# Low parts of the rotated groups made by VectorE one step later in place of GpSimd, and the attention ratio by `tensor_scalar` in place of `scalar_tensor_tensor`

## The chip, the cores and the metric

The kernel runs on one core of one Trainium2 chip. The metric is the time of one execution on the device in microseconds (us); the kernel before has a median of 1994.56 us over three runs (1994.23 to 1994.79). A measurement of this kernel can tell about 0.2% (4 us) from no change.

## What is computed

Eight sequences of 512 tokens by 512 features go through one layer: differential attention with rotary embedding, group normalisation, an output projection, a residual and a layer norm, and then a mixture of eight experts of which each token takes two, with another layer norm. The change is in the attention, of which this is the core (16 heads, 4 groups of keys and values, 32 columns to each half of a head):

```python
q1, q2 = _rope(q1, cos, sin), _rope(q2, cos, sin)
k1, k2 = _rope(k1, cos, sin), _rope(k2, cos, sin)
...
s1 = jnp.einsum('bhtd,bhsd->bhts', q1, k1) * scale + mask
s2 = jnp.einsum('bhtd,bhsd->bhts', q2, k2) * scale + mask
a1 = jax.nn.softmax(s1, axis=-1)
a2 = jax.nn.softmax(s2, axis=-1)
diff = a1 - lam * a2
out = jnp.einsum('bhts,bhsd->bhtd', diff, v)
```

Here `_rope` multiplies by the cosine, and adds the neighbour columns (swapped in pairs) times the sine.

## The kernel before

The attention of the eight sequences (batches) is a software pipeline of 48 steps for each batch: four key/value groups (kv) with 12 units each. A unit is one tile of 128 query rows and, for the tiles 0 and 1, two heads, for the tiles 2 and 3 one head; so 16 of a batch's 48 units have two heads (steps 0 to 3, 12 to 15, 24 to 27, 36 to 39). The order of the work is written out by hand: every engine has its own program, loops over the steps and does, in each step, its part of several units that are at different ages. Engines wait for each other by semaphores that count.

In step s, TensorE makes the scores of unit s into `S` (line 660, mask 664), transposes the mixed probabilities of unit s-3 (675), does a share of the next projection into `prep` (642 to 644), tasks of the batch before, and every few steps the products with the values (688, 691). VectorE does, in this order: `scaled_out` in some steps (1081), `maxes` of unit s (1042), `inverse_sums` of unit s-1 (reciprocals, 1050), `mix` of unit s-2 (1073: `mixed = expd_2 * rho + expd_1`, one `scalar_tensor_tensor` a head), `ratios` of unit s-1 (1059: `rho = -lambda * sum_1 / sum_2`, for the heads of the unit in one `scalar_tensor_tensor`), and then, in the steps of a table, `rotate` (1034, 1035), statistics and tasks of the batch before. ScalarE makes the exponentials (856) and copies the transposes (868).

The projections of queries and keys come in groups of 128 columns, ten a batch (`SEQ`: q2, q3, k1, q4, q5, q6, q7, k0, q0, q1; the last batch has seven). `FILL_STEPS` says in which steps a group's four parts are projected; the last of the four is the step in which it is rotated: 2, 5, 8, 12, 15, 18, 23, 32, 35, 38. A group then goes this way:

- in its step, VectorE multiplies `prep` by the cosine into `turned` (1034) and shuffles it into `swapped` (1035), which frees `prep`;
- GpSimd, in the same step of its own program, multiplies `swapped` by the sine (555) and adds it to `turned` (557);
- two steps later, ScalarE copies `turned` rounded into the high part of `parts` (953, `high_part`), and GpSimd subtracts that from `turned` into the low part (562, `low_part`, waits for `hi_done`, adds to `lo_done`);
- SP stores the high part when `hi_done` says so, the low part when `lo_done` does (461), and when both stores have landed gathers the four blocks of 32 rows into `qT` or `kT` (472, `spread`). 

`turned` is a single buffer: `rotate` of the next group waits for `lo_done` of the group before. TensorE waits, in the first step of each kv (step 12 for the second), for the gathers of the groups that it needs; step 12 needs q2 and q3, which are rotated in steps 2 and 5. SP's queue is one program: while it waits for a low part, its later transfers (weights of the next groups, the residual's rows) stand behind it. GpSimd's program has, beside the rotations and low parts, the copies of the values (549) and the indirect DMAs that scatter the finished rows to the experts (578).

The rotation's three operations and the low part run on VectorE for the three groups of the preamble (1034, 1035, 1415, 1417, 1420). From about 1300 us on the experts and the combination follow, which the change does not touch.

## Time and profile before

| what | value |
|---|---|
| median of three runs | 1994.56 us |
| span of the profiled execution, from the first to the last instruction | 1982.6 us |
| median less span | 12.0 us |
| busy: PE, DVE, ACT, POOL | 1681.3, 1394.1, 1166.2, 578.0 us |
| low parts on POOL (562) | 77, mean 1293 ns |
| rotation on POOL (555, 557) | 77 each, mean 1287 and 1394 ns |
| ratios on DVE (1059) | 384, mean 307 ns |
| mixes on DVE (1073) | 512, mean 681 ns |

PE is TensorE, DVE VectorE, ACT ScalarE, POOL GpSimd, SP the queue of most DMAs. A row of a timeline has the start and the duration in us, the engine, the line of the kernel, the operation, the tile written and the tiles read (buffer numbers left out), the shapes, the count of merged instructions, and in brackets how long the engine was idle before it and what ended that. A row of groups has count, busy us and mean ns, then the idle time before. A row of a line has durations in ns (least, median, greatest). The profiled execution's time outside its span is not in the profile; the table has what the median leaves for it.

### The profile page before, as it was taken

Reading aid. Unit: us, or ns where it says so; the run is one execution under the profiler, and the core shown is the slowest. Engines: PE = TensorE matmul, PEld = TensorE weight load, DVE = VectorE, ACT = ScalarE, POOL = GpSimd, SP = SyncE. Lnnn points to the kernel's source line nnn. Section 1 sums busy time; section 2 is a strip of 40 time slices with the busy share of each in tenths; the row PEclk is TensorE's granted clock in tenths of the full one; section 3 lists DMA queues with packets and bytes.
Section 4 is the critical chain, followed back from the end, with each engine's and each line's share of the span. In section 5 each row is a group of like instructions: output and inputs, shape, how many; then the busy total and the mean of one; then the engine's idle time right before and its main releaser. Section 6 shows DMA issues by size and latency. Waiting matters only on the chain. (4 is left out here: it accounts for less than half of the span.)

```text
span 1982.6 us, 36940 instructions
## 1 busy us (share of the span) xinstructions
PE 1681.3 (85%) x9718; PEld 1251.6 (63%) x9719; DVE 1394.1 (70%) x3225; ACT 1166.2 (59%) x3388; POOL 578.0 (29%) x471
## 2 busy tenths in 40 slices
PE   4878898898899899889889889873999999999800
PEld 3556556656566655656656665543999999999700
DVE  4998888988888988888898898744333333333377
ACT  2777878877788788787887887832222222222133
POOL 0322322522432432241251252012533342100075
PEclk8999999999999999999999999985999999999955
DMA  8764755765574574484575566014533344433187
GB/s 280 229 169 128 202 139 139 213 170 150 170 202 120 160 207 124 133 232 125 149 229 144 139 203 179 24 71 175 164 118 118 109 127 148 132 95 94 65 258 250
DMA packets 141462, 311.40 MB, mean 157 GB/s; under 512 B 16608, under 2 KB 19296, under 8 KB 140160
## 3 DMA queue, kind: packets, MB, share of 16 engines
q1 hardware_dynamic: 111264, 231.64, 41.3%
q0 software_dynamic: 15072, 50.74, 7.7%
q10 hardware_dynamic: 14976, 27.27, 3.6%
q8 instruction: 65, 1.06, 0.2%
q14 instruction: 85, 0.70, 0.1%
HBM read 207.87 MB, written 101.71 MB: 156 GB/s over the span
## 5 line engine op out<-in xcount | busy, mean ns | idle before, releaser
L856 ACT ACTIVATE expd<-S,neg_max 128x128 f32<-128x128 f32 (+3 forms) x1024 | 530.9, 535 | 152.5 <-DVE neg_max L1042 151.3
L1042 DVE TENSOR_REDUCE neg_max<-S 128x2 f32<-128x768 f32 (+3 forms) x384 | 399.5, 1040 | 144.9 <-PE S L664 135.7
L1073 DVE SCALAR_TENSOR_TENSOR mixed<-expd,rho 128x384 f32<-128x384 f32 (+3 forms) x512 | 338.8, 681 | 0.0
L660 PE MATMUL S<-kT,qT 128*128 128x256 f32 (+2 forms) x1024 | 276.7, 373 | 30.0 <-DMA qT<-parts_rows 18.2
L675 PE MATMUL PTp<-ident,mixed 128*128 128x128 f32 x1280 | 211.7, 280 | 57.4 <-DVE mixed L1073 53.0
L868 ACT ACTIVATE probsT<-PTp 128x512 f32<-128x512 f32 (+2 forms) x384 | 205.2, 534 | 91.3 <-PE PTp L675 88.8
L1529 ACT ACTIVATE xT_hi<-xTp 128x512 fp32r<-128x512 f32 x72 | 43.1, 599 | 357.9 <-DVE yo L1710 352.0
L660 PEld LDWEIGHTS S<-kT,qT 128*128 128x128 f32 x1024 | 162.5, 193 | 132.5 <-issue 92.0
L722 PE MATMUL tail<-wo,ctxT 128*128 128x512 f32 x464 | 218.9, 595 | 0.3
L856 ACT ACTIVATION_READ_ACCUMULATOR expd<-S,neg_max 128x1 f32 x1024 | 216.7, 212 | 0.0
L555 POOL TENSOR_TENSOR swapped<-swapped,rope_t 128x512 f32<-128x512 f32 x77 | 99.1, 1287 | 397.2 <-DVE swapped L1035 397.2
L675 PEld LDWEIGHTS PTp<-ident,mixed 128*128 128x128 f32 x1280 | 139.6, 142 | 78.0 <-DVE mixed L1073 74.4
L562 POOL TENSOR_TENSOR parts<-turned,parts 128x512 fp32r<-128x512 f32 x77 | 99.6, 1293 | 271.1 <-ACT parts L953 271.1
L691 PE MATMUL O<-probsT,vals 128*64 128x256 f32 x1280 | 168.5, 393 | 0.0
L642 PE MATMUL prep<-xh,wqk 128*128 128x512 f32 x308 | 141.6, 460 | 7.2 <-DVE swapped L1035 7.1
L1710 DVE COPY yo<-Y 128x512 f32<-128x512 f32 x72 | 49.8, 691 | 121.2 <-PE Y L1654 121.2
L1787 POOL DMA_INDIRECT ya<-expert_out_rows,out_slots x64 | 68.9, 1076 | 208.4 <-PEq L1742 189.2
L664 PE MATMUL S<-maskb,identb 128*128 128x128 bf16 (+1 forms) x768 | 125.1, 245 | 0.0
L644 PE MATMUL prep<-xh,wqk 128*128 128x512 f32 x308 | 123.6, 401 | 0.0
L643 PE MATMUL prep<-xl,wqk 128*128 128x512 f32 x308 | 122.7, 398 | 0.0
L1689 DVE TENSOR_TENSOR xT_lo<-xTp,xT_hi 128x512 fp32r<-128x512 f32 x72 | 49.8, 691 | 100.9 <-ACT xT_hi L1529 100.9
L1059 DVE SCALAR_TENSOR_TENSOR rho<-sums,neg_lam,rsum 128x1 f32<-128x1 f32 (+1 forms) x384 | 117.8, 307 | 0.0
(245 smaller groups left out, 3632.7 us busy)
## 6 DMA issues: line engine op xcount, KB each, us to landing
qT<-parts_rows SPq DMA_DIRECT2D x256, 256.0 KB, 4.5
parts_rows<-parts SPq DMA_DIRECT2D x160, 256.0 KB, 2.8
wqk<-wqk_split SPq DMA_DIRECT2D x75, 512.0 KB, 6.1
xin<-expert_in_rows SPq DMA_DIRECT2D x72, 256.0 KB, 3.0
expert_out_rows<-yo ACTq DMA_DIRECT2D x72, 256.0 KB, 3.2
kT<-parts_rows SPq DMA_DIRECT2D x64, 256.0 KB, 4.2
x<-in_x SPq DMA_DIRECT2D x8, 1024.0 KB, 7.2
x_rows<-x SPq DMA_DIRECT2D x8, 1024.0 KB, 7.3
```

The source lines that it names most:

```text
L642: nc.tensor.matmul(prep[:], w[:, c, 0, :], xh[:, c, :], start=(c == 0), stop=False)
L643: nc.tensor.matmul(prep[:], w[:, c, 0, :], xl[:, c, :], start=False, stop=False)
L644: mm = nc.tensor.matmul(prep[:], w[:, c, 1, :], xh[:, c, :], start=False, stop=(c == DC - 1))
L660: nc.tensor.matmul(S[s % 2][:, k * slot:k * slot + w], qT[kv % 2][:, 2 * h + c, i * P:(i + 1) * P], kT[kv][:, c, 0:w], start=(k % per_bank ...
L664: mm = nc.tensor.matmul(bank[:, :, i * P:(i + 1) * P], identb[:], maskb[:].unsqueeze(1).broadcast_to([P, per_bank, P]), start=False, stop= ...
L675: mm = nc.tensor.transpose(PTp[:, o:o + P], mixed[sl % 3][:, a * 256 + j * P:a * 256 + (j + 1) * P], ident[:])
L691: mm = nc.tensor.matmul(O[half * HD:(half + 1) * HD, 0], vals[kv][:, j, :], probsT[i % 2][:, j, half], start=(j == 0), stop=(j == i), tile ...
L722: mm = nc.tensor.matmul(tail[:], ctxT[par][:, c, i * P:(i + 1) * P], wo[:, c, :], start=(c == 2 * first_q), stop=(c == FC - 1))
L856: ex = nc.scalar.activation(expd[s % 3][:, k * slot:k * slot + w], S[s % 2][:, k * slot:k * slot + w], ACT.Exp, bias=neg_max[s % 3][:, k:k ...
L868: nc.scalar.activation(probsT[i % 2][:, 0:i + 1, half:half + n, pair, :].rearrange("p j a q -> p a j q"), PTp[:, 0:w].rearrange("p (a j q) ...
L1042: nc.vector.tensor_reduce(neg_max[s % 3][:, 0:k], v, AX, ALU.max, negate=True).then_inc(max_ready, 1)
L1073: ins = nc.vector.scalar_tensor_tensor(out=mixed[sl % 3][:, a * 256:a * 256 + w], in0=e2, scalar=rr[:, i, h:h + 1], in1=e1, op0=ALU.mult, ...
```

## The change

GpSimd's `low_part` goes, and VectorE gets one, three steps after the group's step in place of two, ahead of the `rotate` of that step. And `ratios` becomes one `tensor_scalar` a head: its one tensor is the sum, its two scalars the other head half's reciprocal sum and -lambda, both read from memory, one number a partition.

```diff
             def body(b, first, second, last):
                 for s, kv, u in steps(b, first, last):
-                    for idx in fills(s, last, 2):
-                        if SEQ[idx][0] != "v":
-                            low_part(group_no(b, idx), half(b, idx))
                     for idx in fills(s, last, 0):
                         if SEQ[idx][0] != "v":
                             rope(group_no(b, idx), fill_no(b, idx), SEQ[idx][0])
...
+            def low_part(n, r2):
+
+                dve.wait_ge(hi_done, n + 1)
+                nc.vector.tensor_tensor(parts[r2][:, 1, :], turned[:], parts[r2][:, 0, :].bitcast(F32),
+                                        ALU.subtract).then_inc(lo_done, 1)
+
...
                 dve.wait_ge(rsum_step, u + 1)
-                nc.vector.scalar_tensor_tensor(out=rr[:, i, h0:h0 + nh], in0=L[:, i, 0, h0:h0 + nh],
-                                               scalar=neg_lam[:, 0:1], in1=Q[:, i, 1, h0:h0 + nh],
-                                               op0=ALU.mult, op1=ALU.mult).then_inc(rho_step, 1)
+                for h in heads:
+                    ins = nc.vector.tensor_scalar(rr[:, i, h:h + 1], L[:, i, 0, h:h + 1], Q[:, i, 1, h:h + 1],
+                                                  neg_lam[:, 0:1], ALU.mult, ALU.mult)
+                ins.then_inc(rho_step, 1)
...
+                    for idx in fills(s, last, 3):
+                        if SEQ[idx][0] != "v":
+                            low_part(group_no(b, idx), half(b, idx))
                     for idx in fills(s, last, 0):
                         if SEQ[idx][0] != "v":
                             rotate(group_no(b, idx), fill_no(b, idx), SEQ[idx][0])
```

VectorE, before, from the mix of step 4 to the maxima of step 6 (rows give line, operation, tiles and the shape written):

```order
L1073 SCALAR_TENSOR_TENSOR mixed<-expd,rho 128x256 x2
L1059 SCALAR_TENSOR_TENSOR rho<-sums,neg_lam,rsum 128x2
L1042 TENSOR_REDUCE neg_max<-S 128x2
L1050 RECIPROCAL rsum<-sums 128x2
L1073 SCALAR_TENSOR_TENSOR mixed<-expd,rho 128x256 x2
L1059 SCALAR_TENSOR_TENSOR rho<-sums,neg_lam,rsum 128x1
L1034 TENSOR_TENSOR turned<-prep,rope_t 128x512
L1035 STREAM_SHUFFLE swapped<-prep 128x512
L1042 TENSOR_REDUCE neg_max<-S 128x2
```

The same stretch of VectorE with the change:

```order
L1077 SCALAR_TENSOR_TENSOR mixed<-expd,rho 128x256 x2
L1063 TENSOR_SCALAR rho<-sums,rsum,neg_lam 128x1 x2
L1045 TENSOR_REDUCE neg_max<-S 128x2
L1053 RECIPROCAL rsum<-sums 128x2
L1077 SCALAR_TENSOR_TENSOR mixed<-expd,rho 128x256 x2
L1063 TENSOR_SCALAR rho<-sums,rsum,neg_lam 128x1
L1037 TENSOR_TENSOR parts<-turned,parts 128x512
L1031 TENSOR_TENSOR turned<-prep,rope_t 128x512
L1032 STREAM_SHUFFLE swapped<-prep 128x512
L1045 TENSOR_REDUCE neg_max<-S 128x2
```

The ratio of step 4, of a unit of two heads, has become two instructions, that of step 5 is still one; and the low part of q2 (`parts`) stands between the ratio and the rotation of q3.

GpSimd, before, the first two groups of the loop:

```order
L555 TENSOR_TENSOR swapped<-swapped,rope_t 128x512
L557 TENSOR_TENSOR turned<-turned,swapped 128x512
L562 TENSOR_TENSOR parts<-turned,parts 128x512
L555 TENSOR_TENSOR swapped<-swapped,rope_t 128x512
L557 TENSOR_TENSOR turned<-turned,swapped 128x512
L562 TENSOR_TENSOR parts<-turned,parts 128x512
```

GpSimd, with the change, the same two groups and the next:

```order
L555 TENSOR_TENSOR swapped<-swapped,rope_t 128x512
L557 TENSOR_TENSOR turned<-turned,swapped 128x512
L555 TENSOR_TENSOR swapped<-swapped,rope_t 128x512
L557 TENSOR_TENSOR turned<-turned,swapped 128x512
L555 TENSOR_TENSOR swapped<-swapped,rope_t 128x512
L557 TENSOR_TENSOR turned<-turned,swapped 128x512
```

The low part and its wait for ScalarE have left GpSimd's program.

## Rows read from the trace of the kernel before

**Rows 1.** Busy time by stretch: window, us, each engine's busy us (instructions), PEclk, DMA.
```profile
506.00:542.00 36.00, 30.07 (x187) 21.28 (x186) 34.11 (x76) 27.74 (x86) 18.69 (x16) 0.98 0.64 189
558.00:618.00 60.00, 59.59 (x298) 35.84 (x299) 50.36 (x111) 44.58 (x130) 11.75 (x10) 1.00 0.54 149
618.00:663.00 45.00, 39.80 (x291) 30.01 (x289) 39.08 (x109) 37.67 (x109) 10.76 (x11) 1.00 0.56 153
```

**Rows 2.** Waits (us, times, longest): PE in 506 to 663 us, DVE in 558 to 618.
```profile
PE PTp L675 <- DVE mixed L1073: 5.0, 7, 1.1
PE S L660 <- DMA qT<-parts_rows: 1.8, 1, 1.8
...
DVE neg_max L1042 <- PE S L664: 8.0, 9, 2.4
```

**Rows 3.** Timeline, SP's gathers of q3 and PE's first scores of step 12.
```profile
534.09 1.74 SPq L472 DMA_DIRECT2D qT<-parts_rows  x4
...
541.07 0.74 PE L660 MATMUL S<-kT,qT 128*128 128x256 f32 x4 [1.84 <-DMA qT<-parts_rows]
```

**Rows 4.** Timeline of POOL: low part of q2, rotation add and low part of q3.
```profile
518.70 1.29 POOL L562 TENSOR_TENSOR parts<-turned,parts 128x512 fp32r<-128x512 f32 x1 [0.58 <-ACT parts L953]
...
523.52 1.47 POOL L557 TENSOR_TENSOR turned<-turned,swapped 128x512 f32<-128x512 f32 x1
...
528.67 1.29 POOL L562 TENSOR_TENSOR parts<-turned,parts 128x512 fp32r<-128x512 f32 x1 [0.95 <-ACT parts L953]
```

**Rows 5.** Timeline of DVE, steps 4 to 8 of the fourth batch.
```profile
516.83 0.85 DVE L1073 SCALAR_TENSOR_TENSOR mixed<-expd,rho 128x256 f32<-128x256 f32 x2
...
519.00 1.66 DVE L1073 SCALAR_TENSOR_TENSOR mixed<-expd,rho 128x256 f32<-128x256 f32 x2
520.59 0.20 DVE L1059 SCALAR_TENSOR_TENSOR rho<-sums,neg_lam,rsum 128x1 f32<-128x1 f32 x1
520.72 0.68 DVE L1034 TENSOR_TENSOR turned<-prep,rope_t 128x512 f32<-128x512 f32 x1
...
522.86 0.16 DVE L1050 RECIPROCAL rsum<-sums 128x2 f32<-128x2 f32 x1
522.93 0.93 DVE L1073 SCALAR_TENSOR_TENSOR mixed<-expd,rho 128x384 f32<-128x384 f32 x1
523.78 1.22 DVE L1059 SCALAR_TENSOR_TENSOR rho<-sums,neg_lam,rsum 128x1 f32<-128x1 f32 x1
...
530.51 0.65 DVE L1034 TENSOR_TENSOR turned<-prep,rope_t 128x512 f32<-128x512 f32 x1
```

**Rows 6.** The ratios: durations of the line, then its groups by shape.
```profile
L1059 DVE SCALAR_TENSOR_TENSOR rho<-sums,neg_lam,rsum x384: 203/211/1254, 50.7 to 1300.2; 128x1 f32<-128x1 f32 x128, 128x2 f32<-128x2 f32 x64
...
L1059 DVE SCALAR_TENSOR_TENSOR rho<-sums,neg_lam,rsum 128x1 f32<-128x1 f32 x256 | 80.2, 313 | 0.0
...
L1059 DVE SCALAR_TENSOR_TENSOR rho<-sums,neg_lam,rsum 128x2 f32<-128x2 f32 x128 | 37.5, 293 | 0.0
```

**Rows 7.** Timeline: mixes of steps 14, 15, PE in step 16, rotation of step 35.
```profile
549.63 0.58 DVE L1073 SCALAR_TENSOR_TENSOR mixed<-expd,rho 128x128 f32<-128x128 f32 x2
...
552.81 1.06 DVE L1073 SCALAR_TENSOR_TENSOR mixed<-expd,rho 128x128 f32<-128x128 f32 x2
...
558.41 0.66 PE L675 MATMUL PTp<-ident,mixed 128*128 128x128 f32 x4 [0.96 <-DVE mixed L1073]
...
620.79 0.69 DVE L1034 TENSOR_TENSOR turned<-prep,rope_t 128x512 f32<-128x512 f32 x1 [0.53 <-PE prep L644]
```

**Rows 8.** Timeline of DVE in the preamble: a low part and the rotation behind it.
```profile
17.58 0.69 DVE L1420 TENSOR_TENSOR parts<-turned,parts 128x512 fp32r<-128x512 f32 x1
18.37 0.69 DVE L1034 TENSOR_TENSOR turned<-prep,rope_t 128x512 f32<-128x512 f32 x1
```

**Rows 9.** `tensor_scalar` with a pointer operand in the plan: timeline, then the line's durations.
```profile
1352.73 1.26 DVE L1354 TENSOR_SCALAR mixed<-mixed 128x64 f32<-128x64 f32 x7
...
L1354 DVE TENSOR_SCALAR mixed<-mixed x7: 245/254/397, 1352.7 to 1353.7; 128x64 f32<-128x64 f32 x7
```

## The prediction

> **What bounds the kernel now.** I read first the table of busy time by stretch over the fourth of the eight batches (506 to 663 us), which stands for the middle six [rows 1]. The reader is to see two kinds of stretch. In 558 to 618 us (steps 17 to 34) TensorE (PE) is busy 59.59 of 60 us: PE paces, and VectorE (DVE) waits there for scores nine times, 8.0 us [rows 2]. In the first stretch DVE is busy 34.11 of 36 us and PE 30.07: DVE paces. The last stretch is mixed. So work added to DVE costs something in steps 0 to 16 and 35 to 47, and little between.
>
> Next, the waits of PE in the same batch [rows 2]: 5.0 us in seven waits for `mixed`, and one wait of 1.8 us for the gather of `qT`. This one stands at 541.07 us, the first scores of step 12 [rows 3]. They need group q3, whose low part the change moves. GpSimd (POOL) ends it at 528.67 + 1.29 = 529.96 us [rows 4]; SP stores it, issues the gathers from 534.09 us [rows 3], and PE starts 11.1 us after the low part's end. **Step 12 therefore starts 11.1 us after q3's low part, and whatever DVE saves between steps 8 and 12 is hidden.**
>
> Last, the timeline of DVE, with POOL's beside it [rows 4, 5]. Two mixes of 128x256 take 0.85 us in step 4 and 1.66 us in step 5. There POOL's low part runs from 518.70 to 519.99 us, and the mix that began at 519.00 us goes on until it is over. In step 6 the ratio takes 1.22 us where its median is 0.211 us: POOL's rotation add (L557) runs from 523.52 to 524.99 us and the ratio ends at 525.00 us. So a DVE instruction with two SBUF tensors stands still while POOL reads SBUF. The ratios' 384 x 0.211 = 81.0 us against their 80.2 + 37.5 = 117.7 us busy gives 36.7 us of such standing still over the kernel, 4.6 us a batch [rows 6].
>
> By the Trainium skill, "SBUF — State Buffer", section "Who interferes with whom", this is the rule: a VectorE instruction with two SBUF inputs contends with a GpSimd instruction that reads SBUF, and one of the two stands still for the whole instruction of the other. The trace agrees (1.66 against 0.85 us).
>
> **The change, part by part.**
>
> *Low parts leave POOL.* 77 instructions of about 1.3 us go (ten a batch, seven in the last). POOL is 29% busy by the page, so its own time is worth nothing; the relief is on DVE: 1.66 - 0.85 = 0.81 us in step 5 [rows 5], 1.06 - 0.58 = 0.48 us in step 15 [rows 7].
>
> *Low parts enter DVE.* Ten a batch. The same operation stands in the preamble: it takes 0.69 us, and the rotation behind it, which waits for it as it will now, starts 0.79 us after its start [rows 8]. I take 0.79 us where a rotation follows (steps 5, 8, 15, 18, 35, 38), 0.69 us elsewhere. It does not collide with POOL's rotation: the next rotation starts only behind it. Its own wait, for ScalarE's high part, costs nothing: the POOL row that waited for that high part starts at 528.67 us, 1.8 us before DVE is at the place (530.51 us) [rows 4, 5]. If ScalarE were late, the next rotation and all maxima would queue behind it. SP's low store and its gathers move with the low part; behind them in SP's queue stand a load of x and the next projection weights, for neither of which PE waits in this batch [rows 2].
>
> *Ratios.* 384 instructions become 512, since a unit of two heads takes two: 16 more a batch. Price of one: the ratio of before holds DVE for 0.13 us (520.59 us to the rotation at 520.72 us) [rows 5]. The nearest row of a `tensor_scalar` with a pointer operand, 128x64 in the making of the plan, gives (1.26 - 0.25) / 6 = 0.17 us a piece [rows 9], the reciprocal of as few elements 0.07 us (522.86 to 522.93 us) [rows 5]. I take 0.13 us, as it reads pointers and one element, and keep 0.07 and 0.17 as ends. So no change for one head, +0.13 us for two. Relief: if one tensor operand lets it run beside POOL, 1.22 - 0.21 = 1.01 us in step 6, and the like in steps 9, 13 and 19.
>
> **The sum, along the path of one middle batch.**
>
> - Steps 0 to 8, DVE paces: four units of two heads in steps 1 to 4, +0.52; low part of q2 in step 5, +0.79; mix in step 5, -0.81; ratio in step 6, -1.01. Sum -0.51, so DVE reaches the place of q3's low part at 530.51 - 0.51 = 530.00 us and ends it at 530.69 us, against 529.96 us on POOL. **Step 12 starts 0.73 us later.** The ratio saved in step 9 and the low part added in step 11 lie under PE's wait.
> - Steps 12 to 16: PE is delayed by 0.73 already. In step 15 DVE gains 0.48 and pays 0.13 and 0.79, so the mix of step 16 is another 0.44 late, and PE was waiting for that mix (0.96 us at 558.41 us) [rows 7]: **+0.44 us.** The savings in steps 13 and 19 end in waits of DVE for scores: nothing.
> - Steps 17 to 34, PE paces: six edits, nothing on the path. The cover is the 8.0 us that DVE waits there [rows 2]; without it they would cost at most three low parts and four doubled ratios, 2.7 us.
> - Step 35: DVE waits 0.53 us for the projection before its rotation [rows 7]; the low part fits there but for 0.79 - 0.53 = **0.26 us.** Steps 37 to 41: four doubled ratios and two low parts, 2.0 us, against a relieved mix as in step 5 (0.8 us) and waits of DVE for scores: nothing.
>
> Sum 1.43 us a batch. Seven batches (the last lacks step 35): 7 x 1.43 - 0.26 = 9.8 us. In the first batch there is no tail of an earlier batch and the terms are of both signs; costs of 10 x 0.69 + 16 x 0.13 = 9.0 us a batch stand against relief of 4.6 us (ratios) and about as much for mixes; I take nothing, within 3 us. Experts and combination (1300 us on) are untouched. The profiled execution spans 1982.6 us; the median of the runs is 1994.56 us, 12.0 us more, which I carry over: span 1992.4 us, **time 2004.4 us**.
>
> **Rivals.**
>
> 1. *The ratio still stands still* (the second edit does not do what it says). No row shows a `tensor_scalar` of one element beside a POOL read. Then step 6 gives back 1.01 us in seven batches and the first batch about 3 us: 2004.4 + 10 = 2014.5 us. For it: the plan's `tensor_scalar`, with indirect DMAs issued on POOL beside it, takes up to 397 ns against 245 [rows 9]. Against: its median is 254. By the Trainium skill, "VectorE: DVE Perf Modes", section "Mode 2×_2P — use both read ports for one tensor", `tensor_scalar` from SBUF to SBUF reads its one tensor through both ports, so that it too would meet GpSimd; whether one element does is not shown by any row here.
> 2. *Faster: the ratio is short and DVE is the pace everywhere.* At 0.07 us, 512 ratios take 36 us where 384 took 384 x 0.13 = 50 us; with the relief of 36.7 us and a mix relief of about 0.81 + 0.48 and as much again a batch (20 us), 71 us stand against 77 x 0.69 = 53 us: -18 us, if all of it counts; half, by the share of DVE-paced time [rows 1], gives 1985.5 us. It decides at a ratio of 0.09 us and less. Against it: q3's gather bounds steps 8 to 12, and PE the middle.
> 3. *No change.* The low part as cheap as 0.60 us and pairs at 0.10 us bring step 12 to +0.4 us and the others near nothing: +3 us, 1997.5 us. The steps' slack also swallows parts of 1 us.
> 4. *Far slower: q3's gather slips more.* If pairs cost 2 x 0.17 us and rival 1 holds as well, step 12 starts 0.73 + 1.01 + 0.48 (four pairs at 0.08 more, and singles at 0.04) = 2.2 us late, and the rest of the batch 1 us: 24 us, 2019 us.
>
> **How the numbers follow.** A measurement here can tell about 0.2%, 4 us. Forecast 0.40, rival 1 0.22, rival 2 0.14, rival 3 0.16, rival 4 0.08. Faster by over 0.2% (under 1990.6): rival 2, 0.14, and a little from the unknown first batch, 0.15 together. Within: rival 3 and some of the forecast's low edge, 0.22. Slower: 0.63. The likeliest alone is 1999 to 2010 us; the range takes in rivals 1 and 3 whole and rival 4's centre, and leaves out most of rival 2 and the edge above: 1988 to 2021 us.
>
> **What would show it.** DVE rows of the low parts at 0.69 us with a rotation 0.79 us behind, no wait ahead of them; two-head ratios as two rows, 0.13 us apart; ratios' maximum down from 1254 ns to about 250 (forecast) or not (rival 1); mix in step 5 at 0.85 us; PE's wait for `qT` at step 12 grown from 1.8 to over 3 us while batch intervals grow by about 1.4 us. The prediction is wrong if that wait does not grow, if DVE is idle at a low part, or if batches become shorter.

## The result, and the profile after

| | before | with the change |
|---|---|---|
| median | 1994.39 us (4 runs, 1992.22 to 1994.79) | 2026.82 us (4 runs, 2020.31 to 2029.27) |
| ratio, 95% interval | | 1.0152 [1.0125, 1.0178] |
| span of the profiled execution | 1982.6 us | 2018.5 us |
| attention, first to last `maxima` | 46.1 to 1295.7: 1249.6 us | 46.2 to 1327.6: 1281.3 us |

The change costs 32.4 us by the medians, where 10 were forecast and 2021 us was the upper end. The two profiled executions differ by more, 35.9 us of span. Of these, 31.7 us lie in the attention: 23.7 in the six middle batches, 2.0 in the first, 6.0 in the last. The other 4 us lie behind it, in work that no edit touches (686.8 us before, 690.9 with the change, 688 to 698 in the other kernels of this study). All ratios below come from executions at the usual speed; one of `after_mended` (8616 us) and two of the kernel before beside it (2238 and 2267 us) were in a slow state, so that its median counts the first and its ratio none of them.

The busy times of the page's first part:

```profile
PE 1699.0 (84%) x9718; PEld 1263.6 (63%) x9719; DVE 1420.5 (70%) x3430; ACT 1167.6 (58%) x3388; POOL 476.9 (24%) x394
```

The three edited operations: one row from the groups of each, then durations of the lines (least, median, greatest in ns).

```profile
L1077 DVE SCALAR_TENSOR_TENSOR mixed<-expd,rho 128x384 f32<-128x384 f32 (+3 forms) x512 | 313.9, 633 | 0.3 <-issue 0.3
L1063 DVE TENSOR_SCALAR rho<-sums,rsum,neg_lam 128x1 f32<-128x1 f32 x512 | 125.3, 265 | 0.0
L1037 DVE TENSOR_TENSOR parts<-turned,parts 128x512 fp32r<-128x512 f32 x77 | 52.1, 676 | 0.0
...
L1063 DVE TENSOR_SCALAR rho<-sums,rsum,neg_lam x512: 254/266/273, 49.9 to 1332.1; 128x1 f32<-128x1 f32 x171
L1037 DVE TENSOR_TENSOR parts<-turned,parts x77: 653/680/685, 60.8 to 1255.9; 128x512 fp32r<-128x512 f32 x77
```

POOL lost 101 us of busy time and VectorE gained 26: 52.1 for the low parts and 7.6 more for the ratios (125.3 against 80.2 + 37.5 [rows 6]), less 24.9 for the mixes (338.8 us before); rows overlap, so that the groups sum to 8 us more. The greatest ratio fell from 1254 to 273 ns, and no low part takes over 685 ns: nothing edited stands still beside POOL any more.

The stretches of the fourth batch that answer to [rows 1], and then its waits, answering to [rows 2] (TensorE in 515 to 678 us, VectorE in 571 to 631).

```profile
515.00:553.00 38.00, 30.40 (x189) 21.53 (x188) 33.65 (x83) 29.37 (x91) 14.97 (x13) 0.99 0.61 177
571.00:631.00 60.00, 59.70 (x294) 35.54 (x295) 51.73 (x117) 43.50 (x129) 7.84 (x6) 1.00 0.52 144
631.00:678.00 47.00, 41.57 (x291) 30.60 (x290) 40.98 (x114) 38.30 (x109) 6.74 (x7) 0.96 0.53 146
```

```profile
PE PTp L672 <- DVE mixed L1077: 5.2, 7, 1.3
PE S L657 <- DMA qT<-parts_rows: 4.1, 1, 4.1
...
DVE neg_max L1045 <- PE S L661: 7.1, 7, 1.8
```

The first stretch is 2 us longer with less of VectorE in it, and the wait for `qT` has gone from 1.8 to 4.1 us. VectorE from the mix of step 5 on, with both low parts that step 12 waits for:

```profile
528.78 0.85 DVE L1077 SCALAR_TENSOR_TENSOR mixed<-expd,rho 128x256 f32<-128x256 f32 x2
...
529.74 0.68 DVE L1037 TENSOR_TENSOR parts<-turned,parts 128x512 fp32r<-128x512 f32 x1
530.52 0.69 DVE L1031 TENSOR_TENSOR turned<-prep,rope_t 128x512 f32<-128x512 f32 x1
...
533.59 0.26 DVE L1063 TENSOR_SCALAR rho<-sums,rsum,neg_lam 128x1 f32<-128x1 f32 x1
533.77 0.68 DVE L1092 BATCH_NORM_STATS2 bn<-ctxT 128x6 f32<-128x512 f32 x1
...
539.32 0.66 DVE L1037 TENSOR_TENSOR parts<-turned,parts 128x512 fp32r<-128x512 f32 x1
540.09 0.69 DVE L1031 TENSOR_TENSOR turned<-prep,rope_t 128x512 f32<-128x512 f32 x1
```

The mix of step 5 takes 0.85 us where it took 1.66 [rows 5], and the ratio of step 6 0.26 where it took 1.22. The low parts take 0.66 to 0.68 us with the rotation 0.77 to 0.78 us behind. A ratio holds VectorE for 0.18 us (533.59 to 533.77), not 0.13.

Then SP's queue (issues only; the stores are L461, the weights for q4's projection L510), and TensorE's first scores of step 12, with the change:

```profile
534.62 0.34 SPq L510 DMA_DIRECT2D wqk<-wqk_split  x1
537.52 2.88 SPq L461 DMA_DIRECT2D parts_rows<-parts  x2
545.19 1.74 SPq L472 DMA_DIRECT2D qT<-parts_rows  x4
...
552.23 0.73 PE L657 MATMUL S<-kT,qT 128*128 128x256 f32 x4 [4.09 <-DMA qT<-parts_rows]
```

And SP's queue before:

```profile
524.21 0.34 SPq L510 DMA_DIRECT2D wqk<-wqk_split  x1
528.67 1.70 SPq L461 DMA_DIRECT2D parts_rows<-parts  x2
```

Counted from the first maxima of the batch (515.25 us, before 506.14): q3's low part ends 0.9 us later (24.7 against 23.8 us; 0.73 were predicted). But its gathers are issued 2.0 us later (29.9 against 28.0): after 5.2 us instead of 4.1. From the gathers to the scores it is 7.0 us in both. Between the weights and q3's stores there was a gap of 4.5 us before; now it is 2.9, because the weights are issued 1.3 us later in the batch (19.4 against 18.1 us): in SP's program they stand behind q2's stores and gathers, and q2's low part now comes in step 5.

Where a batch got longer: the time between the starts of `maxima` (VectorE's line 1042 before, 1045 with the change), mean of the middle six batches (us), from the timelines of the kernels of this study. Two that moved a load too far, described below, are left out.

| steps | 0-4 | 5-7 | 8-11 | 12-16 | 17-23 | 24-34 | 35-40 | 41-47 | batch |
|---|---|---|---|---|---|---|---|---|---|
| before | 12.04 | 10.50 | 13.42 | 17.12 | 23.70 | 35.75 | 22.58 | 23.73 | 158.84 |
| the change | 12.65 | 9.52 | 15.50 | 17.66 | 24.40 | 35.75 | 23.07 | 24.25 | 162.79 |
| ratio_only | 12.66 | 9.35 | 14.54 | 17.25 | 23.45 | 35.75 | 23.16 | 23.88 | 160.05 |
| low_only | 12.39 | 10.37 | 14.43 | 16.99 | 24.52 | 35.75 | 23.36 | 23.69 | 161.51 |
| after_load_early | 12.74 | 9.50 | 14.19 | 17.68 | 24.40 | 35.76 | 23.08 | 24.16 | 161.51 |
| before_load_early | 12.09 | 10.77 | 12.92 | 17.69 | 23.68 | 35.74 | 22.36 | 23.68 | 158.93 |
| low_not_q2q3 | 12.06 | 10.38 | 13.51 | 17.15 | 24.69 | 35.75 | 22.44 | 23.90 | 159.89 |
| low_behind | 12.20 | 10.19 | 14.80 | 16.56 | 24.66 | 35.75 | 23.77 | 23.77 | 161.70 |
| low_moved | 12.55 | 10.43 | 14.41 | 17.13 | 23.65 | 35.79 | 22.67 | 23.68 | 160.31 |
| ratio_single | 12.17 | 9.46 | 14.58 | 16.95 | 23.68 | 35.74 | 22.59 | 23.84 | 159.01 |
| ratio_single_early | 12.21 | 9.46 | 14.04 | 16.84 | 23.68 | 35.74 | 23.07 | 23.88 | 158.93 |
| after_mended | 12.34 | 9.45 | 15.15 | 17.15 | 23.66 | 35.75 | 22.96 | 23.90 | 160.35 |

A batch of the change is 3.95 us longer: 1.71 up to step 11, 0.54 in steps 12 to 16, 0.70 in 17 to 23, 1.01 from 35 on. The theory that the experiments test has three separate costs, namely (1) q3's chain, with the weights' place on the queue; (2) doubled ratios at 0.18 us; (3) low parts in the middle, where the sum of VectorE's waits did not cover them. The third took its form only after the first eight runs. Where an expectation numbers its theories, 1 is the reading that the time goes into q3's chain and the doubled ratios, and 1a the part of it on the weights' place. The rivals stand with each experiment.

### The profile page after: what moved, and what is told of

Same layout as the page of the kernel before. It is cut to its first block and busy times, and to the rows that moved or that the text cites. A ratio compares the mean times of both kernels' runs of the same rounds, so it can differ in the third digit from the quotient of the medians.

```text
span 2018.5 us, 37128 instructions
## 1 busy us (share of the span) xinstructions
PE 1699.0 (84%) x9718; PEld 1263.6 (63%) x9719; DVE 1420.5 (70%) x3430; ACT 1167.6 (58%) x3388; POOL 476.9 (24%) x394
## 5 line engine op out<-in xcount | busy, mean ns | idle before, releaser
L1077 DVE SCALAR_TENSOR_TENSOR mixed<-expd,rho 128x384 f32<-128x384 f32 (+3 forms) x512 | 313.9, 633 | 0.3 <-issue 0.3
L657 PE MATMUL S<-kT,qT 128*128 128x256 f32 (+2 forms) x1024 | 278.2, 374 | 37.0 <-DMA qT<-parts_rows 28.1
L672 PE MATMUL PTp<-ident,mixed 128*128 128x128 f32 x1280 | 215.9, 285 | 61.2 <-DVE mixed L1077 57.8
L639 PE MATMUL prep<-xh,wqk 128*128 128x512 f32 x308 | 144.5, 469 | 15.6 <-DVE swapped L1032 10.8
L1063 DVE TENSOR_SCALAR rho<-sums,rsum,neg_lam 128x1 f32<-128x1 f32 x512 | 125.3, 265 | 0.0
L641 PE MATMUL prep<-xh,wqk 128*128 128x512 f32 x308 | 124.9, 405 | 0.0
L719 PEld LDWEIGHTS tail<-wo,ctxT 128*128 128x128 f32 x464 | 79.8, 190 | 61.3 <-issue 58.3
```

What stands on the lines that cost most here:

```text
L639: nc.tensor.matmul(prep[:], w[:, c, 0, :], xh[:, c, :], start=(c == 0), stop=False)
L641: mm = nc.tensor.matmul(prep[:], w[:, c, 1, :], xh[:, c, :], start=False, stop=(c == DC - 1))
L657: nc.tensor.matmul(S[s % 2][:, k * slot:k * slot + w], qT[kv % 2][:, 2 * h + c, i * P:(i + 1) * P], kT[kv][:, c, 0:w], start=(k % per_bank ...
L672: mm = nc.tensor.transpose(PTp[:, o:o + P], mixed[sl % 3][:, a * 256 + j * P:a * 256 + (j + 1) * P], ident[:])
L719: mm = nc.tensor.matmul(tail[:], ctxT[par][:, c, i * P:(i + 1) * P], wo[:, c, :], start=(c == 2 * first_q), stop=(c == FC - 1))
L1063: ins = nc.vector.tensor_scalar(rr[:, i, h:h + 1], L[:, i, 0, h:h + 1], Q[:, i, 1, h:h + 1], neg_lam[:, 0:1], ALU.mult, ALU.mult)
```

## The experiments

### The two edits apart

**ratio_only** is the kernel before with the second edit alone. **low_only** is the change with the ratio of before.

ratio_only, against the kernel before:

```diff
-                nc.vector.scalar_tensor_tensor(out=rr[:, i, h0:h0 + nh], in0=L[:, i, 0, h0:h0 + nh],
...
+                for h in heads:
+                    ins = nc.vector.tensor_scalar(rr[:, i, h:h + 1], L[:, i, 0, h:h + 1], Q[:, i, 1, h:h + 1],
+                                                  neg_lam[:, 0:1], ALU.mult, ALU.mult)
+                ins.then_inc(rho_step, 1)
```

> The kernel before with the ratio by tensor_scalar alone; the low part stays on GpSimd. Theory 1 (both edits cost): a tensor_scalar with two pointers holds VectorE for 0.18 us (the trace after the change), so 512 x 0.18 - 384 x 0.13 = 42 us of VectorE are added against 36.7 us of standing still beside GpSimd that go, spread unevenly: the costs in steps 1 to 4, 13 to 16, 25 to 28 and 37 to 40, the relief in steps 6, 9, 13 and 19. Time 1996 to 2008 us, wait of TensorE for qT at step 12 as before (about 1.5 us). Theory 2 (the low part alone is the cause): within 4 us of before or faster, 1980 to 1998 us.

> The changed kernel with the ratio as before (one scalar_tensor_tensor); the low part is on VectorE. Theory 1: step 12 of seven batches starts about 1.9 us later as with the whole change (13 us), and the rest about 1 us a batch: 2010 to 2018 us; ratios stand still up to 1.25 us again. Theory 2: 2024 to 2030 us, all of the loss.

Measured: ratio_only 2007.17 us, 1.0055 [1.0036, 1.0074]; low_only 2014.47 us, 1.0090 [1.0055, 1.0124]. The two add up to 1.45% of the change's 1.52%. Each edit alone makes the kernel slower. In ratio_only the microsecond of step 6 is won (steps 5 to 7: 9.35 against 10.50 us) and lost again in steps 8 to 11 (14.54 against 13.42), and steps 0 to 4, with their doubled ratios, are 0.62 us longer. Both times lie in the range of theory 1, but two of its details failed: in ratio_only TensorE waits longer for `qT` over the kernel (24.2 us in nine waits, 18.2 before), and in low_only step 12 starts 1.23 us later and not 1.9.

### The weights on SP's queue

The weights for q4's projection are moved past q3's gathers (late), or ahead of q2's gathers (early), in both kernels. Late:

```diff
-                    if not (last and idx + 2 >= THIS_BATCH):
+                    if idx != 1 and not (last and idx + 2 >= THIS_BATCH):
                         sp.dma_start(wqk[idx % 2][:].bitcast(F32), wsplit_dram[:, (idx + 2) % NGRP]).then_inc(w_in[idx % 2], 16)
...
                     spread(kind, j, group_no(b, idx), half(b, idx), stack_total(b, idx), free)
+                    if idx == 1 and not (last and idx + 2 >= THIS_BATCH):
+                        sp.dma_start(wqk[idx % 2][:].bitcast(F32), wsplit_dram[:, (idx + 2) % NGRP]).then_inc(w_in[idx % 2], 16)
```

Early, in `spread`, between q2's two stores and the wait for them (`between` issues the load):

```diff
+                if between is not None:
+                    between()
                 at_least(sp, scores_ready, free)
                 apart(sp)
                 sp.wait_ge(parts_out[r2], total // 2)
```

> The changed kernel, with the weights that SP loads for group q4 issued behind the gathers of q3 and not ahead of its stores. Theory 1a (the stores of q3 take 5 to 6 us because that load, now 1.3 us later, lies in front of them): the stores land within 3 us of their issue, step 12 starts 1 to 2.5 us earlier than with the change, time 2010 to 2020 us. Theory 1b (the stores are slow for another reason, or the low part's own lateness is all): step 12 and the time stay, 2023 to 2030 us. If the weights come too late for step 13, TensorE waits there for them and the time is over 2030 us.

> The kernel before with the same move of the weights' load. Theory 1a: the stores of q3, 3.8 us from issue to landing before, land within 3 us, the wait of 1.2 to 2.2 us at step 12 shrinks by about 1.2 us in seven batches: 1984 to 1990 us. Theory 1b: 1992 to 1997 us.

Measured: 2095.56 us, 1.0490 [1.0454, 1.0526], and 2061.36 us, 1.0336 [1.0302, 1.0370]. As experiments on step 12 both miss: q4's projection begins in step 9, not in step 12, and TensorE now waits for its weights. The wait lines of TensorE, of after_load_late and then of before_load_late:

```profile
PE prep L641 <- DMA wqk<-wqk_split: 84.5, 8, 11.2
```

```profile
PE prep L644 <- DMA wqk<-wqk_split: 66.7, 8, 9.1
```

Still they show one thing: without the load ahead of them, q3's gathers of before_load_late go out 2.6 us after the low part's store was issued in the fourth batch (24.34 to 26.98 us of the batch), where it was 4.0 us before. In after_load_late it is 3.45 us, where the change has 5.1.

> The changed kernel, with SP issuing the weights of q4 (wanted in step 9) between the stores and the gathers of q2 in place of behind those gathers; the load is then over before q3's stores. Theory 1a (that load, pushed back by q2's later low part, stands in front of q3's stores): gathers of q3 issued within 2.8 us of the low store (4 to 5 us with the change), step 12 starts 1.3 to 2.5 us earlier in the middle batches, time 2007 to 2017 us. Theory 1b (the stores are slow whatever the load does): 2022 to 2030 us.

> The kernel before with the same earlier load. Theory 1a: step 12 is bounded by the same stores there, 4.0 us from the low store to the gathers; with 2.6 us the wait of 1.2 to 2.2 us nearly goes, 7 x 1.3 us: 1982 to 1990 us. Theory 1b: 1992 to 2000 us.

Measured: after_load_early 2016.72 us, 1.0112 [1.0094, 1.0131], 10 us less than the change; before_load_early 1992.71 us, 1.0006 [0.9981, 1.0032]. SP's queue and step 12's scores in after_load_early, whose fourth batch begins at 513.6 us:

```profile
529.32 0.32 SPq L513 DMA_DIRECT2D wqk<-wqk_split  x1
...
535.79 2.89 SPq L461 DMA_DIRECT2D parts_rows<-parts  x2
542.25 1.74 SPq L474 DMA_DIRECT2D qT<-parts_rows  x4
...
549.41 0.73 PE L664 MATMUL S<-kT,qT 128*128 128x256 f32 x4 [1.41 <-DMA qT<-parts_rows]
```

The low part ends no earlier, but its gathers go out at 28.6 us of the batch instead of 29.9, and TensorE waits 1.41 us instead of 4.09. Steps 8 to 11 lose 1.31 us, others stay: of the 1.71 us up to step 11, 1.24 us (37.67 against 36.43) hang on the weights' place. In the kernel before, the same edit wins 0.5 us in steps 8 to 11 and loses 0.27 in steps 5 to 7 and 0.57 in steps 12 to 16; that expectation, a faster kernel, failed. With the weights early in both kernels, the change's step 12 comes 0.65 us later (36.43 against 35.78 us).

The store did not get as short as expected, though: from the low store to the gathers the fourth batch still takes 3.9 us, not 2.8. The weights are not the only traffic. From the third batch on, GpSimd scatters finished rows by indirect DMAs (578) in steps 0 to 7. The last three, 0.79 MB of packets, are in flight beside q3's stores, and the DMA engines are busy for 0.91 of the stretch from 537.5 to 544 us of the change, between the first of these stores and the gathers. The second batch has no such transfers. From the issue of q3's low store to its gathers (us; the last three kernels are described further down):

| | before | the change | before_load_early | after_load_early | before_load_late | after_load_late | ratio_single | ratio_single_early | after_mended |
|---|---|---|---|---|---|---|---|---|---|
| second batch | 3.50 | 3.56 | 2.49 | 2.54 | 2.11 | 2.10 | 4.09 | 2.99 | 2.76 |
| third to seventh, mean | 4.02 | 4.82 | 3.44 | 3.57 | 2.45 | 3.51 | 4.66 | 4.33 | 4.32 |

So the early weights are worth 1.0 us in the second batch with and without the change, and up to 1.25 us in the others; in the batches with the scatter the same kernel needs up to 1.6 us more. The low part's move also changes this traffic: it stood ahead of the last of the three transfers in GpSimd's program. Before, that one goes out together with q3's low store (530.05 us); with the change it goes out 2.1 us ahead of it (540.07 us). The row before, then with the change:

```profile
530.11 1.12 POOL L578 DMA_INDIRECT expert_in_rows<-x,idx  x1 [0.16 <-issue]
...
537.93 0.97 POOL L578 DMA_INDIRECT expert_in_rows<-x,idx  x1 [0.30 <-issue]
```

In the third to seventh batch of every kernel in which GpSimd makes q3's low part, q3's gathers go out within 0.6 us of the last packet of the scatter, mostly 0.1 us ahead of it; in every kernel in which VectorE makes it, 0.85 to 1.8 us behind it. This points to the scatter as a second part of the cost. No run moved those transfers, so it is not shown.

### Where the low parts cost

**low_not_q2q3** leaves q2's and q3's low parts on GpSimd. **low_behind** has two `turned` buffers, and from k1 on the low part behind the next rotation instead of ahead of it. **low_moved** puts two low parts where VectorE waits in any case. All start from low_only. low_not_q2q3, VectorE (GpSimd keeps its two, two steps behind the rotation as before):

```diff
                     for idx in fills(s, last, 3):
-                        if SEQ[idx][0] != "v":
+                        if idx >= 2 and SEQ[idx][0] != "v":
```

low_behind (q2's and q3's low parts stay ahead of the rotation):

```diff
                     for idx in fills(s, last, 0):
                         if SEQ[idx][0] != "v":
-                            rotate(group_no(b, idx), fill_no(b, idx), SEQ[idx][0])
+                            rotate(group_no(b, idx), fill_no(b, idx), SEQ[idx][0], half(b, idx))
+                    for idx in fills(s, last, 3):
+                        if idx >= 2 and SEQ[idx][0] != "v":
+                            low_part(group_no(b, idx), half(b, idx))
```

low_moved (the group rotated in step 15 has the number 4, that of step 18 the number 5):

```diff
-                    for idx in fills(s, last, 3):
-                        if SEQ[idx][0] != "v":
+                    for idx in range(NGRP):
+                        lag = {4: 2, 5: 5}.get(idx, 3)
+                        if SEQ[idx][0] != "v" and idx in fills(s, last, lag):
                             low_part(group_no(b, idx), half(b, idx))
```

> The ratio as before; the low parts of q2 and q3 stay on GpSimd two steps later, the other eight groups' on VectorE three steps later. Theory 1 (about half of the low part's cost is the later start of step 12): steps 0 to 11 take 36.0 to 36.3 us again (37.3 with all low parts on VectorE), the rest as there; time 2003 to 2008 us. Rival (VectorE's added work alone costs, wherever it lies): 2010 to 2015 us, as the work of eight groups in ten is still there.

> The ratio as before; low parts on VectorE, with two buffers of the rotated group, so that from k1 on the low part stands behind the next group's rotation and not ahead of it (q2 and q3 as in the change). Theory 1 (in steps 15, 18 and 35 the low part holds up the rotation, and TensorE waits for its bank of projections): steps 17 to 23 take 23.8 to 24.1 us in place of 24.5, and steps 35 to 40 22.6 to 23.0 in place of 23.4; time 2006 to 2011 us. Rival (it is VectorE's time, whatever the order): as with the low part ahead, 2012 to 2017 us; slower still if the low part now stands against GpSimd's rotation.

Measured: low_not_q2q3 2009.85 us, 1.0079 [1.0049, 1.0110], between the ranges of the theory and of its rival; low_behind 2010.57 us, 1.0072 [1.0047, 1.0097]. The time of low_behind lies in its theory's range, but its batch is no shorter than that of low_only (161.70 against 161.51 us). Steps 0 to 11 of low_not_q2q3 are those of before (35.95 against 35.96 us; low_only 37.19): the early steps pay for q2's and q3's low parts and for no others. Steps 17 to 23 stay at 24.7 us in both kernels. So it is neither a late start of the batch nor the rotation's place behind the low part; the second of these had been the theory of low_behind, which fell.

What it is shows when the timelines of steps 18 to 23 are laid side by side. Before (VectorE's rotation of step 18 and the `ctxT` behind it, TensorE's product with the values in its step 19, the mix of step 22 and its transposes in TensorE's step 23):

```profile
564.21 0.69 DVE L1034 TENSOR_TENSOR turned<-prep,rope_t 128x512 f32<-128x512 f32 x1 [0.23 <-PE prep L644]
...
564.74 1.88 PE L722 MATMUL tail<-wo,ctxT 128*128 128x512 f32 x4
...
565.45 0.41 DVE L1081 TENSOR_TENSOR ctxT<-O,scale 128x256 f32<-128x256 f32 x1
...
566.46 0.38 PE L688 MATMUL O<-ident,rwide 128*128 128x128 f32 x2
...
576.76 0.73 DVE L1073 SCALAR_TENSOR_TENSOR mixed<-expd,rho 128x512 f32<-128x512 f32 x1
...
577.84 0.61 PE L675 MATMUL PTp<-ident,mixed 128*128 128x128 f32 x4
```

The same in low_only, with the low parts of steps 18 and 21:

```profile
573.84 0.69 DVE L1037 TENSOR_TENSOR parts<-turned,parts 128x512 fp32r<-128x512 f32 x1
574.63 0.69 DVE L1031 TENSOR_TENSOR turned<-prep,rope_t 128x512 f32<-128x512 f32 x1
574.68 1.88 PE L719 MATMUL tail<-wo,ctxT 128*128 128x512 f32 x4
...
575.87 0.41 DVE L1084 TENSOR_TENSOR ctxT<-O,scale 128x256 f32<-128x256 f32 x1
...
576.55 0.43 PE L685 MATMUL O<-ident,rwide 128*128 128x128 f32 x2
...
585.02 0.68 DVE L1037 TENSOR_TENSOR parts<-turned,parts 128x512 fp32r<-128x512 f32 x1
...
587.77 0.73 DVE L1076 SCALAR_TENSOR_TENSOR mixed<-expd,rho 128x512 f32<-128x512 f32 x1
...
588.56 0.66 PE L672 MATMUL PTp<-ident,mixed 128*128 128x128 f32 x4 [0.17 <-DVE mixed L1076]
```

In step 18 VectorE had 0.23 us to spare, and the low part needs 0.79. `ctxT`, which frees the accumulator `O`, ends at 576.28 us, 1.60 us after TensorE began the `tail` products (before: 565.86, 1.12 us). TensorE's next product follows the start of `tail` by 1.87 instead of 1.72 us. The same wait has a line of its own among the waits of steps 17 to 23 in low_not_q2q3:

```profile
PE O L688 <- DVE ctxT L1087: 0.3, 1, 0.3
```

In step 21 VectorE had nothing to spare, and the mix of step 22 comes 0.17 us too late by the profile. Measured from TensorE's first scores of a step to those of the next (mean of the six batches), low_only is longer than before in steps 19, 20 and 23, by 0.18, 0.28 and 0.37 us, and equal from step 24 to 34. This is what low_moved was made for; its expectation counts these steps of TensorE one lower.

> low_only (low parts on VectorE, ratio as before) with two low parts moved to where VectorE waits anyway: that of the group rotated in step 15 goes from step 18 to the end of step 17 (the 1.6 us wait for scores of step 18), that of the group rotated in step 18 goes from step 21 to step 23 (ahead of its 1.2 us wait). Read by TensorE's first scores of step 17 to those of step 24, mean of the middle six batches: before 22.48 us, low_only 23.30. Theory (the cover is local: in steps 18 and 21 VectorE has 0.2 us of slack or none, and TensorE waits 0.2 to 0.4 us in steps 18, 19 and 22; the 8 us of waits lie in other steps): back to 22.4 to 22.7 us, and the time some 5 us under low_only's 2014.5, 2005 to 2012. Rival (the low parts cost by their sum, or TensorE is slowed by something else): 23.1 us or more, 2013 to 2018.

Measured: 2006.38 us, 1.0078 [1.0049, 1.0108]. From TensorE's scores of step 18 to those of step 25 it takes 22.43 us (before 22.48, low_only 23.30), and steps 17 to 23 by VectorE's maxima 23.65 (23.70, 24.52). The intervals of the whole time overlap with those of low_only, so that the steps decide here and not the time. The same two low parts, at their new places:

```profile
570.61 0.69 DVE L1037 TENSOR_TENSOR parts<-turned,parts 128x512 fp32r<-128x512 f32 x1 [1.14 <-ACT parts L950]
...
588.78 0.69 DVE L1037 TENSOR_TENSOR parts<-turned,parts 128x512 fp32r<-128x512 f32 x1
...
591.18 0.69 DVE L1045 TENSOR_REDUCE neg_max<-S 128x4 f32<-128x512 f32 x1 [0.25 <-PE S L661]
```

The first fills a stretch in which VectorE had nothing to do (it waited 1.14 us for the high part, where before it waited for scores), and behind the second VectorE still waits for scores. VectorE does as much work as in low_only, and the two cost nothing. The theory of the local cover holds.

### The relief of the ratio

**ratio_single** gives the `tensor_scalar` to units of one head alone; **ratio_single_early** moves the weights as well, as in the early kernels.

```diff
+                if nh > 1:
...
+                else:
+                    nc.vector.tensor_scalar(rr[:, i, h0:h0 + 1], L[:, i, 0, h0:h0 + 1], Q[:, i, 1, h0:h0 + 1],
+                                            neg_lam[:, 0:1], ALU.mult, ALU.mult).then_inc(rho_step, 1)
```

> The kernel before with the ratio by tensor_scalar for units of one head alone; units of two heads keep the one scalar_tensor_tensor. Theory (the loss of ratio_only came from the doubled instruction of two-head units, and the relief beside GpSimd is real): steps 0 to 4 as before (12.0 us between maxima, ratio_only 12.7), steps 5 to 7 1 us shorter (9.4), and q3's low part up to 1 us earlier, so steps 0 to 11 together some 0.5 us shorter than before's 35.96: 1986 to 1993. Rival (the tensor_scalar costs 0.05 us more in each unit, and what is gained stays under q3's stores and gathers): 1993 to 2002, steps 8 to 11 longer by what steps 5 to 7 gain.

> ratio_single, and SP issues q4's weights between q2's stores and q2's gathers, as in before_load_early. Theory (with the weight load out of the way of q3's stores, the microsecond won in step 6 brings step 12 forward): steps 0 to 11 at 34.5 to 35.3 us (before 35.96, before_load_early 35.78), time 1980 to 1990. Rival (given back in steps 12 to 16, as in before_load_early, 17.69 against 17.12): steps 12 to 16 at 17.7 or more, 1989 to 1997.

Measured: ratio_single 1992.90 us, 1.0011 [0.9988, 1.0035]; ratio_single_early 1992.15 us, 1.0013 [0.9992, 1.0034]: both are the time of before, and neither expectation of a gain held. Steps 0 to 4 are back (12.17 us), so the doubled instruction was ratio_only's loss there. The microsecond of step 6 is won, and steps 8 to 11 take it back (14.58 against 13.42). Its way is seen in ratio_single's fourth batch, which begins at 512.1 us:

```profile
530.25 0.34 SPq L510 DMA_DIRECT2D wqk<-wqk_split  x1
533.79 1.86 SPq L461 DMA_DIRECT2D parts_rows<-parts  x2
...
533.93 1.30 POOL L562 TENSOR_TENSOR parts<-turned,parts 128x512 fp32r<-128x512 f32 x1
...
540.21 1.74 SPq L472 DMA_DIRECT2D qT<-parts_rows  x4
```

The low part ends at 23.1 us of the batch, 0.7 us earlier than before, and the gathers still go out at 28.1 us (before 28.0). The stores come nearer to the weights, but that is not all that holds them: with the weights early as well, q3's low part ends 0.65 us earlier than in before_load_early (23.32 against 23.97 us, mean of six), and the gathers go out 0.17 us later (27.51 against 27.34). In the second batch, without GpSimd's scatter, they do go out 0.37 us earlier; in the others they leave, as before, 0.1 us ahead of the last packet of that scatter. What takes the microsecond back is thus narrowed to the DMA traffic and not shown. Steps 8 to 11 of ratio_single_early shrink by 0.54 us against ratio_single, but its batch is that of before (158.93 against 158.84 us): its steps 35 to 40 are 0.5 us longer, for which see the last section.

### The change mended

**after_mended** joins the early weights, low_moved and ratio_single on the changed kernel (the diffs above).

> The change with the three named costs taken out together: q4's weights ahead of q2's gathers (as in after_load_early), the two low parts of steps 18 and 21 moved to steps 17 and 23 (as in low_moved), and units of two heads with one scalar_tensor_tensor (as in ratio_single). Theory (three separate costs that add): a middle batch of 162.8 us in the changed kernel less 1.3 (weights), 0.85 (low parts of steps 18 and 21) and 0.7 to 1.0 (doubled ratios) is 159.6 to 160.0 us, some 1 us above before's 158.8; time 1996 to 2004. Rival (the costs are one slack spent thrice, so that mending the first leaves nothing to the others): a batch of 161 us or more, 2008 to 2017.

Measured: 2000.99 us, 1.0035 [1.0017, 1.0052], a batch of 160.35 us. By the ratios about 25 of the 32 us are gone, and the time is where the theory had it. The batch is 0.35 us over its interval: steps 8 to 11 are at 15.15 us, between 13.6 and 16.8 in single batches, where after_load_early has 14.19. So the first cost did not come out as fully as in after_load_early. The 13.6 us are those of the second batch, where q3's gathers follow the low store after 2.76 us; in the third to seventh they need 4.32 us, with the weights long out of the way. GpSimd's scatter is the likeliest reason, and it is open. No kernel of this study is faster than the kernel before beyond what a measurement can tell.

## Why the prediction was right in direction and too small

- **"the path of one middle batch": what held.** The price of a low part (0.69 predicted, 0.66 to 0.68 measured; 0.79 and 0.77 to the rotation), the relief of the mixes and of the ratio (1.01 predicted, 0.96 in step 6), and the low part's wait for ScalarE at no cost. The size of steps 12 to 16 came close (0.44 against 0.54 us), but no run bears out its terms: low_only, with the low part and the relieved mix, has -0.13 us there, ratio_only, with the pairs, +0.13, and before_load_early, with neither, +0.57. PE's wait for `qT` grew from 1.8 to 4.1 us, the sign that was named for it.
- **"Step 12 starts 0.73 us later": mis-sized, 1.71 us in the mean.** q3's low part came 0.9 us later, near enough. The step that failed was the sentence that behind the low store in SP's queue stand transfers "for neither of which PE waits", and the fixed 11.1 us from the low part to step 12. One of these transfers, the load of weights, is pushed back by q2's low part and then runs ahead of q3's stores. after_load_early shows it: 1.24 of the 1.71 us. With the weights early in both kernels 0.65 us are left, near the predicted 0.73. The prediction also left out the transfers of GpSimd, which share the DMA engines with q3's stores; their part is not shown.
- **"Price of one: 0.13 us".** Measured 0.18, just above the upper end of 0.17: a doubled pair costs 0.23 us more than the one instruction did. At 0.05 us more for each of 64 instructions a batch this is 3.2 us of VectorE's time a batch more than predicted, most of it hidden. What the pairs cost on the path is 0.49 us in steps 0 to 4 (12.66 in ratio_only against 12.17 in ratio_single). The batches differ by 1.04 us in all (160.05 against 159.01), but 0.57 of it lies in steps 35 to 40, where four batches against two met a lower clock (below).
- **"Steps 17 to 34, PE paces: six edits, nothing on the path."** This failed too: 0.70 us a batch, all in steps 17 to 23. (The edits are seven by the prediction's next sentence, three low parts and four pairs.) The cover named, 8.0 us of VectorE's waits, is a sum over 60 us; the low parts of steps 18 and 21 stand where 0.23 us and nothing are to spare. The end that the prediction gave "without the cover", 2.7 us, was a bound on the right thing. low_moved shows it: same work, other steps, no cost.
- **Steps 35 to 47: 0.26 predicted, 1.01 measured.** In the batches whose steps 35 to 40 run undisturbed they take 22.5 us against 22.1, so 0.4 of these are the change's; 0.1 in the mean is the clock (below). The 0.5 us in steps 41 to 47 appear neither in low_only (-0.04) nor fully in ratio_only (+0.15), and after_mended has 0.17 of them. No run took them apart; they stay open.
- **"In the first batch ... nothing, within 3 us."** +2.0 us. The last batch, counted like the others less step 35 (1.2 us), lost 6.0, 3.5 of them in steps 8 to 11.
- **"12.0 us more, which I carry over".** This was wrong too: the profiled run of the change took 2020.31 us with a span of 2018.5, so 1.8 us lie around a span, and the profiled execution of before must have been one of about 1984 us, faster than any of its four timed ones. The error falls out of the comparison, as the median rose by 32.4 and the span by 35.9 us.
- **Rivals.** The first, that the ratio still stands still, is refuted: no `tensor_scalar` takes over 273 ns, though 38 of the 512 overlap a `tensor_tensor` of GpSimd. By the Trainium skill, "VectorE: DVE Perf Modes", section "Mode 2×_2P — use both read ports for one tensor", a `tensor_scalar` from SBUF to SBUF can read its one tensor through both read ports, and so would meet GpSimd as well; with one element to read, the rows here show no such meeting. The second (faster) needed a ratio under 0.09 us. The third needed pairs of 0.10 us. The fourth had the right place, q3's gather, and came nearest in time (2019 us), but by the wrong cause.

## What to carry to other kernels

In this kernel an engine's waits covered added work only in the step where they stand: lay the new instruction into the timeline, and look at the wait just behind it, not at the sum of a stretch. When an operation moves, follow every queue that it passes to the next transfer that something waits for, since a load that nobody waits for can stand ahead of one that somebody does; and look at what other queues move at that time. And a microsecond saved ahead of a fixed chain is worth what the chain lets through: here q3's stores took that much longer and nothing came of it.

## What the runs showed of the hardware

- **A `tensor_scalar` of one element with two pointers takes 254 to 273 ns and holds VectorE for 0.18 us**, a `scalar_tensor_tensor` with one pointer 0.13 us, a reciprocal 0.07 us [rows 5]. Beside a `tensor_tensor` of GpSimd, 38 of the 512 took at most 270 ns; a `scalar_tensor_tensor` in these places took up to 1254 ns [rows 6].
- **A busy TensorE can hide waits of 0.2 to 0.4 us.** The stretch 571 to 631 us shows 59.70 of 60 us busy, though in the mean of the six batches steps 19, 20 and 23 are longer than before by 0.22, 0.30 and 0.42 us. Before, the rows of TensorE overlap there by 0.16 us (`tail` ends at 566.62 us, the next product starts at 566.46; the profile models these ends); in low_only that overlap is gone (576.56, 576.55), and the wait is not listed. Intervals between the same rows of neighbouring steps show it.
- **The same wait of TensorE is followed by 1.1 to 1.7 us more in some batches.** In step 39 of every middle batch TensorE waits 1.8 to 1.9 us for `ctxT`. The rows of two batches of the change, the wait and the stretch (PEclk is the column before the last two):

```profile
647.53 0.66 PE L728 MATMUL tail<-ident,x 128*128 128x128 f32 x4 [1.84 <-ACT ctxT L897]
...
809.88 0.63 PE L728 MATMUL tail<-ident,x 128*128 128x128 f32 x4 [1.93 <-ACT ctxT L897]
```

```profile
646.70:652.60 5.90, 5.07 (x28) 2.87 (x29) 3.35 (x7) 4.86 (x15) 2.55 (x2) 0.71 0.74 177
808.90:813.60 4.70, 3.63 (x28) 2.27 (x28) 3.70 (x8) 4.47 (x15) 2.55 (x2) 1.00 0.69 173
```

  The first has a granted clock of 0.71 over the stretch, which is more than half of it at 1.2 GHz, the second 1.00, all of it at 2.4 GHz. From the scores of step 39 to those of step 40 it is 5.7 to 5.8 us in the undisturbed batches and 6.8 to 7.4 in the others, with nothing between. Of the middle six the kernel before has two such batches, the change three, low_only five, ratio_single two, ratio_single_early four. So the differences in steps 35 to 40 between kernels are for the most part a count of these, and say little on the edits. What decides whether the clock falls after this wait no run shows.
